# Storing a ring slot directly behind its own gathers in two spline convolutions of a graph network

## What is computed

```python
def spline_conv(x, row, col, basis, idx, W, b):
    z = jnp.einsum('ni,kio->nko', x, W).reshape(N * K, Fout)      # K = 125
    gathered = z[col[:, None] * K + idx]
    msg = jnp.einsum('es,eso->eo', basis, gathered)
    out = jax.ops.segment_sum(msg, row, num_segments=N)
    deg = jax.ops.segment_sum(jnp.ones_like(msg[:, 0]), row, num_segments=N)
    return out / jnp.maximum(deg, 1.0)[:, None] + b
h = jax.nn.elu(spline_conv(h, row, col, basis, idx, stn1_w, stn1_b))
h = jax.nn.elu(spline_conv(h, row, col, basis, idx, stn2_w, stn2_b))
h = jax.nn.elu(h @ stn3_w + stn3_b)
t = h @ stn4_w + stn4_b
new_pseudo = jnp.clip(pseudo + t[col] - t[row], 0.0, 1.0)
basis2, idx2 = spline_basis(new_pseudo)
return spline_conv(x, row, col, basis2, idx2, conv_w, conv_b)
```

## Time and profile before

| | us |
|---|---|
| median of 3 runs | 13724.47 |
| lowest and highest run | 13675.15, 13794.92 |
| span of the profiled execution | 13681.2 |
| PE busy | 7155.1 (52%) |
| DVE busy | 7727.2 (56%) |
| ACT busy | 2965.5 (22%) |
| POOL busy | 7334.9 (54%) |

### The profile page before, as it was taken

One profiled execution on the slowest core, in us unless ns is written; L12 is line 12 of the kernel. 1 busy time (PEld: TensorE's weight loads), 2 busy tenths in 40 slices (PEclk: granted clock), 3 DMA queues, 4 the chain that ended last, 5 costly groups with the idle time before them and its releaser, 6 DMA issues. The chain is left out here.

```text
span 13681.2 us, 203231 instructions
## 1 busy us (share of the span) xinstructions
PE 7155.1 (52%) x48670; PEld 6010.6 (44%) x48670; DVE 7727.2 (56%) x17337; ACT 2965.5 (22%) x9191; POOL 7334.9 (54%) x7456
## 2 busy tenths in 40 slices
PE   3466666664765777777899455555555500000000
PEld 2355555553664566555688444344455400000000
DVE  9744444443775445444577444343367546777777
ACT  0011111111222233222344222222234200010001
POOL 4256555552004888888400678777700066666663
PEclk9866666666887888888999656565588655555555
DMA  1200000006223333333322233232222211112121
GB/s 38 86 2 2 2 2 2 2 2 9 31 31 70 77 79 81 75 77 76 70 57 57 46 49 49 45 48 46 48 44 42 28 41 48 52 49 53 49 53 43
DMA packets 1774339, 603.40 MB, mean 44 GB/s; under 512 B 1584837, under 2 KB 1715365, under 8 KB 1774050
## 3 DMA queue, kind: packets, MB, share of 16 engines
q1 hardware_dynamic: 1062354, 307.85, 11.2%
q0 software_dynamic: 255648, 274.30, 9.8%
q10 hardware_dynamic: 456304, 20.89, 2.8%
HBM read 429.15 MB, written 172.95 MB: 44 GB/s over the span
## 5 line engine op out<-in xcount | busy, mean ns | idle before, releaser
L1187 PE MATMUL c_acc<-c_spread_sb,c_basis_sb 128*125 128x256 f32 (+1 forms) x12544 | 2813.1, 388 | 1026.1 <-issue 422.0
L1187 PEld LDWEIGHTS c_acc<-c_spread_sb,c_basis_sb 128*125 128x125 f32 x12544 | 2331.1, 234 | 1420.1 <-issue 722.1
L1554 POOL DMA_INDIRECT at_ring<-gat_table,at_place x1568 | 1583.9, 1010 | 1478.5 <-issue 1478.5
L606 POOL DMA_INDIRECT rec<-rk_rec,rk_place x1568 | 1615.2, 1030 | 1108.8 <-DVE rk_place L496 617.8
L942 POOL DMA_INDIRECT c_ring<-hid_table,c_at x1568 | 1638.8, 1045 | 478.7 <-issue 457.8
L942 POOL DMA_INDIRECT c_ring<-feat_table,c_at x1568 | 1562.7, 997 | 477.8 <-issue 464.1
L1061 DVE TENSOR_TENSOR c_spread_sb<-c_mark,c_rin 128x512 f32<-128x512 f32 (+1 forms) x3136 | 1745.3, 557 | 53.8
L1273 ACT ACTIVATE c_sums<-c_acc 125x512 f32<-125x512 f32 (+1 forms) x3136 | 1446.4, 489 | 1499.1 <-PE c_acc L1187 1135.8
L1201 PE MATMUL c_mix<-c_sums,c_w 125*64 125x128 f32 (+1 forms) x18816 | 1292.3, 304 | 539.7 <-issue 411.6
L1201 PEld LDWEIGHTS c_mix<-c_sums,c_w 125*64 125x64 f32 (+1 forms) x18816 | 1006.8, 140 | 828.6 <-issue 655.3
L1811 PE MATMUL gr_hps<-ident,gr_hs 128*32 128x128 f32 x98 | 29.9, 409 | 2469.5 <-issue 1907.8
(11 more groups left out here) (357 smaller groups left out, 10706.8 us busy)
## 6 DMA issues: line engine op xcount, KB each, us to landing
c_rin<-rows SPq DMA_DIRECT2D x3136, 42.0 KB
c_rin<-rows SPq DMA_DIRECT2D x3136, 20.0 KB
rows<-c_ring POOLq DMA_DIRECT2D x392, 128.0 KB
rows<-rk_blank SPq DMA_DIRECT2D x112, 252.0 KB
rows<-c_ring POOLq DMA_DIRECT2D x392, 72.0 KB
rows<-at_ring SPq DMA_DIRECT2D x196, 144.0 KB
rec<-rk_rec,rk_place POOLq DMA_INDIRECT x1568
c_ring<-hid_table,c_at POOLq DMA_INDIRECT x1568
```

What stands on the lines that cost most here:

```text
L606: pool.indirect_dma_start(out=d.rec, out_offset=bass.IndirectOffsetOnAxis(ap=place[:, u, j:j + 1], axis=0), in_=rec[:, u, j, :], in_offset ...
L1187: last = pe.matmul(acc[pp % BANKS][:, (w % 2) * WN * feats:(w % 2 + 1) * WN * feats], basis[:, q, w, :, :].rearrange("p a b -> p (a b)"), ...
L1554: pool.indirect_dma_start(out=ring[:, u, j, :], out_offset=None, in_=d.gat_table, in_offset=bass.IndirectOffsetOnAxis(ap=place[:, u, j:j + ...
```

## The change

Each slot is stored directly behind its own gathers. Its `done` is raised one slot later, where it was two slots later before. At the end of the phase the two extra steps fall away.

```diff
                     gather_slot(h, u)
                     if u == 2 and not last:
                         take_places(t + 1, 1 - h)
+                    store_slot(t, u)
                     if not (first and u == 0):
-                        store_slot(t if u else t - 1, (u - 1) % RING)
-                    if not (first and u < 2):
-                        slot_done(t if u >= 2 else t - 1, (u - 2) % RING)
+                        slot_done(t if u else t - 1, (u - 1) % RING)
...
             turn_of_slots(turns - 1, (turns - 1) % 2, last=True)
-            store_slot(turns - 1, RING - 1)
-            slot_done(turns - 1, RING - 2)
             slot_done(turns - 1, RING - 1)
```

## The result

The changed kernel takes 13943.73 us (median of 4 runs, 13929.1 to 13969.94), the kernel before 13711.65 in the same comparison. The ratio of the two on record is 1.0125, with a 95% interval of 1.0079 to 1.017; the medians themselves, one divided by the other, give 1.0169. A second comparison, made later, gave 1.0202 (1.016 to 1.0244). The change makes the kernel slower by one to two per cent.

A forecast was written before the change was run, and what follows sets the result against it. The consuming chain bounds both phases before, POOL after. A 2.28 us wait per slot leaves 95 us beyond POOL's slack; 75 us for nearly equal chains makes +170: 13681 to 13851, or 13895 us on the median; range 13680 to 14300.

The forecast's parts named there:

- The wait in each slot: POOL between a slot's last gather and its store: 1.55 us landing plus 0.73 us behind the event, 2.28 us a slot.
- The way to the end: End of c2 and c3: most of the wait falls into POOL's slack; 27 and 68 us remain, together 95 us.
- The toll: Consuming chain beside gathers: pays 9.1 us (c2) and 10.9 us (c3) per turn, however spread; near-equal chains add 75 us.
- Short wait: Rival: POOL's waits are only 2.10 and 2.06 us, the consuming chain stays the bound; 0 to +60 us; chance 0.30.
- By time: Rival: blocks stay at 38.7 and 39.9 us as long as gathers run; +726 us, about 14450; chance 0.10.
- Long landing: Rival: every slot waits as long as a phase's last, 4.47 and 4.19 us; about 15430 us; chance 0.05.
- Faster: Rival: pauses free the consuming chain by more than their length and gathers collide less; 13430 us; chance 0.07.
- break-even: Slot time over which POOL sets a phase's end: 8.39 us in c2, 8.10 us in c3.
- The skill's figure: Gather's landing by the skill's page: 1.14 us behind its end; slots 0.41 us shorter, POOL not the bound.

The follow-up runs named there:

- the store behind one gather: Against the kernel before, each slot's store stands behind the first gather of the next slot: 12904.71 against 13095.44 us; on another chip 13048.17 against 13781.49.
- one wait for two slots: The changed kernel, but POOL gathers two slots (eight gathers), waits once, then issues both stores: 13581.72 us, ratio 0.9885 to the kernel before.
- stores behind one and two gathers in turn: Against the kernel before, stores stand alternately behind the first and the second gather of the next slot: 12882.81 us, ratio 0.933.
- a wait of like length in both phases: The order before, but POOL awaits each store's landing right behind its issue: 13986.95 us, ratio 1.0689 to the kernel before.

## Why the prediction was right

The direction and the mechanism came out as forecast: POOL becomes the bound of both phases because it stands still for each landing. The size was near: 1.24% against 1.25% in the first comparison and 2.0% in the second. That the first two agree to a hundredth is luck: the medians lie 1.7% apart and the profiled spans 2.1%, and two terms of the sum were off, in opposite directions.

- **The wait in each slot.** Forecast 2.28 us, measured 2.35. For the 714 stores that waited for the landing it was 2.22; the 70 at every eleventh slot, which no row of before showed, waited 1.37 us longer each, 96 in all. (From the last gather's end, with the copy of places where there is one, the mean is 2.41.) Read event by event over four stretches of 300 to 600 us, the landing took 1.5 to 1.6 us in the mean, as forecast, and the store started 0.7 to 0.8 us behind its event, except at the eleventh slots, where it was 2.1. So the term that was too small is the time behind the event. The slots came out at 8.60 and 8.49 us (from the first slot's start to the last one's) instead of 8.46 and 8.27, about 140 us more over both phases. The gathers themselves hardly changed. (In the prediction's working of that term, 6701.62 - 6701.1 is 0.52, not 0.55; with the 0.2 beside it that is still about 0.73.) Of the two bounds the lower one, taken from the steady loop, was the right neighbourhood; the landings at the phases' ends (4.2 to 4.5 us) were no measure for the loop. At the end of the changed kernel's phases such long landings stand again:

```profile
7605.21 0.80 POOL L949 DMA_DIRECT2D rows<-c_ring  x1 [5.49 <-DMA c_ring<-hid_table,c_at]
...
10994.38 0.80 POOL L949 DMA_DIRECT2D rows<-c_ring  x1 [6.09 <-DMA c_ring<-feat_table,c_at]
```

- **The way to the end.** POOL as the bound of both phases with its slack used up gave +95 us. With the slots as measured the same sum gives about 235, and the longer waits of the two last slots (5.49 and 6.09 us) another 7, against the 244 measured.
- **The toll.** The forecast let the consuming chain pay 9.1 and 10.9 us for each turn of gathers, however far apart, and added 75 us because the two chains would then be almost equally slow. That step failed. SP waited 10.6 us for `done` in each block and no longer for the spreading, and with the store behind one gather the chain kept up with 30.0 and 29.1 us a block, on a chip where before takes 13781. No row shows the 75 us; they made up for part of the missing 140. Read on its own profile the forecast was 170 us and the phases cost 244.
- **The rivals.** *Short wait* fell: its 2.10 and 2.06 us lie under even the 2.22 of the ordinary stores. *By time* fell: blocks became faster, 34.0 us. (What was said against it isn't so: in the slot above, the gathers are still landing for 1.45 of the 2.17 us in which POOL stands still.) *Long landing* fell. *Faster* was wrong for this change, since a slot of 8.5 us lies above the break-even of 8.39 and 8.10. A part of its mechanism was right, however: the consuming chain can be freed by more than the gathers thin out, and at 7.2 to 7.5 us a slot that gives 5 to 7% where before takes 13781. It isn't the pause that does it: eight gathers with a pause behind them gave nothing in c2, and a store behind every second gather did it without one.
- **The skill's figure.** An estimate by the Trainium skill (DMA: Bandwidth & Descriptors, Anatomy of one DMA — SWDGE (gpsimd) path) put the landing 1.14 us behind a gather's end. In the slot above the event came 1.45 us behind it, and the measurement decides.

What relieves the consuming chain is narrowed down, not explained. Four gathers and a store, without a pause, hold c2's blocks at 37.5 to 39.1 us; eight gathers with a pause behind them at 38.3; runs broken by a store after two, or by a standstill of 1 us in four, let them go at 29.5 to 30. The length of a run isn't all: runs of five and three at 7.17 us a slot go faster than runs of four at 6.40. Pace and order were held apart in one pair only. One place where the loss shows is the mixing. First its row in the kernel with one wait for two slots, then in the one with stores behind one and two gathers in turn (columns: busy us, mean ns, idle before, what ended most of it):

```profile
L1202 PE MATMUL c_mix<-c_sums,c_w 125*64 125x128 f32 (+1 forms) x18816 | 1372.6, 319 | 684.9 <-issue 486.1
```

```profile
L1203 PE MATMUL c_mix<-c_sums,c_w 125*64 125x128 f32 (+1 forms) x18816 | 1204.4, 291 | 420.4 <-issue 333.0
```

The spans of these two differ by 735 us (13619.8 and 12884.9), and this one line by 433: 168 us more busy time and 264 more idle time ahead of it, 153 of that put down to issue, in which PE waited for nothing visible. The longer busy time goes with the lower clock in the windows above (0.85 against 0.95 in c2, 0.70 against 0.76 in c3). What the idle time at issue is (late instructions, say) is open: no run took it apart, and 333 us of it are left in the fastest kernel too.

## What to carry to other kernels

A wait moved behind its own transfer costs the whole landing plus the time to go on (here 2.35 us with 1.45 of landing), and it counts only from the point at which its engine's slack is used up: compute that break-even first, phase by phase. Then look whether the chain that bounds the kernel pays for the other one's traffic; if it does, slowing the engine with slack can be a gain. In this study the fastest kernel was one whose gathers in c2 end 136 us before c3 begins, where they ended 889 us before it at first. How transfers follow each other can matter as well as how many there are in a time.

## What the runs showed of the hardware

- At the same pace of POOL in c2, 7.1 to 7.2 us a slot, the other chain took 38.3 us a block beside gathers in runs of eight and 29.5 beside runs of five and three. One pair shows it, and in its slower kernel the stores also come two by two.
- TensorE's granted clock was higher where blocks came faster: in c2 0.84 before (39.1 us a block), 0.91 in the changed kernel (34.0) and 0.95 in the fastest (29.5). The levels behind these means are 1.2 and 2.4 GHz.
- Before a store that waits for the gathers directly ahead of it POOL stood idle for 2.22 us in the mean in 714 of 784 slots, with 1.45 us of landing in the slot shown. In the other 70, one in eleven, it was 3.59 us; no run took apart why.
- The same kernel took 13095 us on one chip and 13748 and 13781 on two others, while POOL's slots in the order before went alike wherever they were profiled (6.04 to 6.13 us in c3). In the one phase in that order that was profiled on the first of these chips (c3, with the change in c2 alone) it was the blocks that came faster, 30.2 us against 37.2 and 40.0. So a change that makes POOL the bound costs 1 to 2% on one chip and may cost more on another: on the fast one the change in c2 alone cost 2.3% in its single run, and a wait of like length in both phases 6.9%. The whole change wasn't run there.
